# Sums of batches 5 and 6 ahead of the projection and scores of batch 7, and small steps moved to other engines

## The reference

```
xn  = layernorm(x)
qh, kh, vh = xn Wq^T, ctx Wk^T, ctx Wv^T
s   = causal(qh kh^T / 16);  p = softmax(s, axis=1)        # over the query axis
x1  = x + tanh(g_xattn) * (p vh)
xn2 = layernorm(x1)
xq  = clip(round(xn2 / sx)) ;  sx = sigmoid(clip_x) * max|xn2| / 127   # over all batches
h   = silu(xq Wg^T) * (xq Wu^T)      # weights quantised by row
out = x1 + tanh(g_ffn) * (quantised(h) Wd^T)
```

## Time and profile before

| | |
|---|---|
| median of the runs | 106.55 us |
| the profiled execution | 106.31 us |
| its span, first to last instruction | 104.5 us |
| TensorE clock granted | 1.00 throughout (the 2.4 GHz level) |
| PE busy | 96.9 us (93%) |
| DVE busy | 80.6 us (77%) |
| ACT busy | 66.1 us (63%) |
| POOL busy | 43.6 us (42%) |

### The profile page before, as it was taken

One profiled execution on the slowest core, in us unless ns is written; L12 is line 12 of the kernel. 1 busy time (PEld: TensorE's weight loads), 2 busy tenths in 40 slices (PEclk: granted clock), 3 DMA queues, 4 the chain that ended last, 5 costly groups with the idle time before them and its releaser, 6 DMA issues.

```text
span 104.5 us, 1739 instructions
## 1 busy us (share of the span) xinstructions
PE 96.9 (93%) x562; PEld 75.1 (72%) x564; DVE 80.6 (77%) x210; ACT 66.1 (63%) x125; POOL 43.6 (42%) x78
## 2 busy tenths in 40 slices
PE   7799999999999999999999987999999697899990
PEld 2268988988889898897878975444444386889970
DVE  0544296497998999597597979559999998879991
ACT  0421071657972755636738978789888989799800
POOL 6030335047083583508517594055696560350000
PEclk9999999999999999999999999999999999999999
DMA  2999999999354010010985500000000000005555
GB/s 51 333 371 336 376 422 419 419 407 401 138 6 44 0 45 9 23 34 0 150 154 116 110 0 0 0 6 3 0 0 0 0 0 0 0 6 192 209 201 201
DMA packets 11176, 13.54 MB, mean 130 GB/s; under 512 B 6432, under 2 KB 7712, under 8 KB 11168
## 3 DMA queue, kind: packets, MB, share of 16 engines
q1 hardware_dynamic: 10304, 12.39, 37.9%
q10 hardware_dynamic: 864, 1.05, 3.2%
HBM read 10.09 MB, written 2.10 MB: 117 GB/s over the span
## 4 chain that ended last, share of the span: by engine, by line
PE 47%; DVE 20%; DMA 16%; POOL 5%; issue 4%; ACT 3%; SPq 1%; DVEq 0%; POOLq 0%
PE ps L465 9%; DVE hmax L1100 9%; PE ps L686 9%; DMA spread<-rstd 8%; PE ps L503 5%; PE ps L485 5%; DMA r_wide<-spread 5%; DMA wk_sb<-in_wk 4%; DVE shared L1095 4%; PE ps L635 2%; POOL shared L436 2%; PE ps L523 2%; PE ps L540 2%; PE ps L691 2%; PE ps L516 2%
## 5 line engine op out<-in xcount | busy, mean ns | idle before, releaser
L635 PE MATMUL ps<-xq,wguT 128*128 128x512 bf16 x78 | 17.2, 379 | 0.7 <-DVE xq L1075 0.6
L436 POOL TENSOR_TENSOR shared<-up_sb,silu 128x1024 f32<-128x1024 f32 x5 | 11.8, 2366 | 9.5 <-ACT up_sb L830 9.5
L635 PEld LDWEIGHTS ps<-xq,wguT 128*128 128x128 bf16 x80 | 7.8, 98 | 9.8 <-issue 0.6
L465 PE MATMUL ps<-wvT,shared 128*128 128x256 f32 x56 | 13.3, 381 | 0.0
L485 PE MATMUL ps<-shared,a_sb 128*128 128x256 f32 x56 | 13.2, 379 | 0.0
L1100 DVE TENSOR_REDUCE hmax<-shared 128x1 f32<-128x2048 f32 (+1 forms) x6 | 12.7, 2109 | 0.6
L825 ACT ACTIVATE silu<-ps,gu_scale 128x1024 f32<-128x1024 f32 x10 | 11.2, 1115 | 2.1 <-PE ps L635 2.1
L503 PEld LDWEIGHTS ps<-uT,shared 128*128 128x128 f32 x64 | 10.7, 190 | 2.2 <-DVE uT L892 1.0
L503 PE MATMUL ps<-uT,shared 128*128 128x256 f32 (+1 forms) x64 | 12.0, 330 | 0.2 <-DVE uT L892 0.2
L465 PEld LDWEIGHTS ps<-wvT,shared 128*128 128x128 f32 x56 | 10.6, 190 | 1.8 <-DMA shared<-in_xc 0.4
L686 PE MATMUL ps<-hq,wdT 128*128 128x256 bf16 x80 | 10.6, 273 | 0.3 <-DVE hq L1135 0.3
(11 more groups left out here) (120 smaller groups left out, 188.4 us busy)
## 6 DMA issues: line engine op xcount, KB each, us to landing
shared<-in_xc SPq DMA_DIRECT2D x6, 512.0 KB, 10.8
out<-xn SPq DMA_DIRECT2D x7, 256.0 KB, 2.0
xs<-in_x SPq DMA_DIRECT2D x3, 512.0 KB, 8.4
shared<-in_wgu SPq DMA_DIRECT2D x3, 512.0 KB, 7.8
wd<-in_wd SPq DMA_DIRECT2D x1, 896.0 KB, 11.8
shared<-in_xc SPq DMA_DIRECT2D x3, 256.0 KB, 6.9
xs<-in_x ACTq DMA_DIRECT2D x2, 256.0 KB, 5.4
r_wide<-spread SPq DMA_DIRECT2D x4, 128.0 KB, 4.7
```

The source lines that it names most:

```text
L436: nc.gpsimd.tensor_tensor(hid[:, 2 * i + 1, :], up_sb[i % 2][:], silu1[i % 2][:], ALU.mult).then_inc(hid_done[1], 1)
L465: last = nc.tensor.matmul(values_bank(b, k), ctxT(b)[:, e, k * P:(k + 1) * P], weights[:, e, :], start=(e == 0), stop=(e == KT - 1))
L635: last = nc.tensor.matmul(bank(4 * half + 2 * g + c), wguT[:, i, g, k, :], xq[:, k, col:col + CH], start=(k == 0), stop=(k == KT - 1))
```

## The change

It has five parts, all in the handling of batches 5, 6 and 7.

1. TensorE: `attend` of 5 stands before the projection of 7, and `attend` of 6 before the scores of 7. Transposes of batch 0 stand between the identity products and the sum of 7.
2. VectorE: residual and statistics of 5 ahead of the scaled queries of 7, residual and statistics of 6 ahead of the row maximum of 7.
3. GpSimd forms `neg_dev` of batch 6 instead of ScalarE, and VectorE takes its largest value ahead of the statistics of 7, not behind them.
4. ScalarE makes the second half of the down weights' integers after the values of 6 and casts that half itself; GpSimd casts the first half alone.
5. SyncE issues the DRAM writes of batches 6 and 7 before the broadcast reads of both.

```diff
-            for b in range(WIDE_FROM, B):
+            def deviation_to_dram(b):
                 n = b - WIDE_FROM
                 sp.wait_ge(rstd1_done, b + 1)
-                sp.dma_start(spread[n], rstd1[:, b]).then_inc(spread_out, 16)
-                sp.wait_ge(spread_out, 16 * (n + 1))
+                sp.dma_start(spread[n], rstd1[:, b]).then_inc(spread_out[n], 16)
+
+            def deviation_to_all(b):
+                n = b - WIDE_FROM
+                sp.wait_ge(spread_out[n], 16)
...
+            for b in range(WIDE_FROM, LAST - 1):
+                deviation_to_dram(b)
+                deviation_to_all(b)
+            deviation_to_dram(LAST - 1)
+            deviation_to_dram(LAST)
+            deviation_to_all(LAST - 1)
+            deviation_to_all(LAST)
...
# GpSimd
-                    pool.wait_ge(wdint_done, KT)
-                    nc.gpsimd.tensor_copy(wd_q[:], wd_i16[:]).then_inc(wd_q_done, 1)
+                    pool.wait_ge(wdint_done, 1)
+                    nc.gpsimd.tensor_copy(wd_q[:, 0], wd_i16[:, 0]).then_inc(wd_q_done[0], 1)
...
+            pool.wait_ge(mv2_done, LAST)
+            for t in range(QT):
+                nc.gpsimd.tensor_scalar(neg_dev[:, t, :], xs[:, NT - 2 * QT + t, :], mv2[:, LAST - 1, t, 0:1], -1.0,
+                                        ALU.subtract, ALU.mult).then_inc(neg_dev6_done, 1)
...
# TensorE
             scores(LAST - 1)
+            attend(LAST - 2)
             project_queries(LAST)
-            attend(LAST - 2)
+            attend(LAST - 1)
             scores(LAST)
-            attend(LAST - 1)
             values_tile(LAST, 1).then_inc(v_done, 1)
...
+            transposes2(0)
             pe.wait_ge(exp_done, B)
...
-            for b in (0, 1, 2, 4, 5):
+            for b in (1, 2, 4, 5):
                 transposes2(b)
...
# ScalarE
-                if b == 5:
-                    quantise_down_weights(1)
             exponentials(LAST - 1)
             values_out(LAST - 1)
+            quantise_down_weights(1)
+            act.wait_ge(wdint_done, KT)
+            nc.scalar.copy(wd_q[:, 1], wd_i16[:, 1]).then_inc(wd_q_done[1], 1)
...
-            act.wait_ge(mv2_done, LAST)
-            for t in range(QT):
-                nc.scalar.activation(neg_dev[:, t, :], xs[:, NT - 2 * QT + t, :], ACT.Identity,
-                                     bias=mv2[:, LAST - 1, t, 0:1], scale=-1.0).then_inc(neg_dev_done, 1)
...
# VectorE
             row_max(LAST - 1)
             largest2(LAST - 3)
+            residual(LAST - 2)
+            invert_sum(LAST - 1)
+            stats2(LAST - 2)
             scale_queries_whole(LAST)
-            invert_sum(LAST - 1)
-            residual(LAST - 2)
-            stats2(LAST - 2)
             variance2(LAST - 2)
+            residual(LAST - 1)
+            stats2(LAST - 1)
             row_max(LAST)
+            variance2(LAST - 1)
...
-            residual(LAST - 1)
-            stats2(LAST - 1)
-            variance2(LAST - 1)
             largest2(LAST - 2)
...
+            dve.wait_ge(neg_dev6_done, QT)
+            largest_deviation(0, QT)
```

More of the change, by code:

```diff
@@ L225, in gated_block @@
         rbc_ready = sem("rbc_ready")
-        spread_out = sem("spread_out")
+        spread_out = [sem(f"spread_out{b}") for b in range(WIDE_FROM, B)]
         r_wide_here = [sem(f"r_wide_here{b}") for b in range(WIDE_FROM, B)]
@@ L258, in gated_block @@
         wdint_done = sem("wdint_done")
-        wd_q_done = sem("wd_q_done")
+        wd_q_done = [sem(f"wd_q_done{t}") for t in range(KT)]
+        neg_dev6_done = sem("neg_dev6_done")
         wguT_here = sem("wguT_here")
@@ L342, in _ @@
                                        wgu_q[:, s].rearrange("p n d -> p (n d)")).then_inc(wguT_here, 16)
-            sp.wait_ge(wd_q_done, 1)
             for t in range(KT):
+                sp.wait_ge(wd_q_done[t], 1)
                 sp.dma_start_transpose(wdT[:, :, t * P:(t + 1) * P], wd_q[:, t]).then_inc(wdT_here, 16)
@@ L418, in _ @@
                 pool.wait_ge(rstd2_done, b + 1)
-                pool.wait_ge(neg_dev_done, QT * (b - LAST + 2))
+                if b == LAST - 1:
+                    pool.wait_ge(neg_dev6_done, QT)
+                else:
+                    pool.wait_ge(neg_dev_done, QT)
                 for t in range(QT):
@@ L1037, in _, with largest_deviation @@
                 nc.vector.reciprocal(inv_sum[:, LAST, k:k + 1], row_sum[:, LAST, k:k + 1]).then_inc(inv_sum_done, 1)
-            residual(LAST - 1)
-            stats2(LAST - 1)
-            variance2(LAST - 1)
             largest2(LAST - 2)
+            def largest_deviation(n0, n1):
+                nc.vector.tensor_reduce(xmax[:, B - 2 + n0:B - 2 + n1], neg_dev[:, n0:n1, :], AX.X, ALU.max,
+                                        apply_absolute_value=True).then_inc(xmax_done, n1 - n0)
+            dve.wait_ge(neg_dev6_done, QT)
+            largest_deviation(0, QT)
             for t, bk in enumerate((RB, SC)):
@@ L1047, in _ @@
                 nc.vector.bn_aggr(mv2[:, LAST, t, :], bn2[:, LAST, t, :]).then_inc(mv2_done, 1)
[L1048 to L1051, removed]
+            for t in range(QT):
+                dve.wait_ge(neg_dev_done, t + 1)
+                largest_deviation(QT + t, QT + t + 1)
             dve.wait_ge(xmax_done, B - 2 + 2 * QT)
```

## The result

The changed kernel took 107.39 us (median of 8 runs, 106.73 to 108.01), the kernel before 106.38 us (8 runs). The ratio is 1.0095 with a 95% interval of 1.0073 to 1.0117: slower by 1.0 us. The forecast was 106.2 us, and the range ended at 107.1. The profiled execution's span is 105.4 us against 104.5.

What follows compares the result with a forecast made beforehand. TensorE was taken as last at the max product's barrier; closing its gap gains 0.49 at best, 0.33 with a 0.06 wait and 0.10 load. Taking 0.38 from 106.31 gives 105.93, plus 0.24 makes 106.2 us; range 105.6 to 107.1.

Steps and rivals of the forecast that it cites:

- the term for GpSimd's new pair: GpSimd's two instructions for the deviations of 6: 0.96 us together, 1.10 as upper bound, from 56.24 to 57.2 or 57.35.
- The cover: Time between the end of GpSimd's pair and VectorE's largest-value step of 6 at 57.49: 0.14 to 0.29 us.
- The slow-pair rival: GpSimd's pair at 0.82 us each, VectorE 0.39 late, gain 0.1, 106.45 us; chance 0.24 shared with another rival.
- the prediction's last 0.36 us: From GpSimd's inverse deviation of 7 ending at 60.37, over the final maximum (60.40 to 60.68), to TensorE's start at 60.73.
- the no-change side: Outcome that the kernel's time reads as the same, within about 0.5% (0.53 us); chance 0.55.
- the late broadcast: Rival: write of 7 and transposes slow the broadcast of 6 to 7.1 us, everything 1.1 later, 107.3 us; chance 0.12.
- The gain of 0.38: Whole kernel: forecast saving in us, taken between 0.49 at best and 0.33; chance of the forecast 0.54.
- TensorE was the last, by 0.14 us: Barrier before the max product at 61.21: VectorE's largest values were done at 61.07, GpSimd's inverse deviation at 60.46.
- TensorE's gap of 0.49 us: Around the scores of 7: they began 0.39 us late and exposed a weight load, 1.41 instead of 1.30; at most 0.49 gained.
- TensorE's stop before the sum of 7 and the exposed load: TensorE waiting for batch 7's first values tile, 57.15 against 57.14: a stop of some 0.06 us and 0.10 of load.
- Nothing is given back there: Behind the max product: first silu loses 0.1 of the gain, but the second waits for TensorE and times the rest.
- The thinnest cover: Values of 6 on ScalarE have their first tile at 52.30, the sum of 6 wants it at 52.37: 0.07 us.

Runs made afterwards that it cites:

- e0: Kernel before plus sixteen GpSimd instructions at the end of its stream, eight operation pairs each twice on 128x256 f32; 108.74 us in one run.
- e1: Changed kernel with GpSimd forming mean minus x as x times -1 plus the mean; 106.44 us, ratio to before 0.9971 to 1.0030.
- e9: e1 with the transposes of batch 0 back behind the sum of 7; 106.52 us, ratio to before 0.9995 to 1.0041.
- e7: Kernel before with the fifth part alone, both DRAM writes first; 106.35 us, ratio to before 0.9984 to 1.0020.
- e8: e1 with statistics of 6 split around the row maximum of 7 and transposes of batch 2 behind the max product; 106.37 us.
- e5: e1 with the DRAM writes and broadcasts of 6 and 7 in their old order; 106.37 us, ratio to before 0.9986 to 1.0029.

## Why the prediction was wrong

**The step that failed** is the term for GpSimd's new pair: "I take 0.96, the same form, with 1.10 as the upper bound". It measured 2.28. The form in the code was a subtract and a multiply; the rows that I took for "its neighbours" were add with multiply, and multiply with multiply. No row of the trace showed a subtract on GpSimd, so neither number was a bound. The operation was in the diff, and I matched the rows by size and number of columns alone. e0 and e1 settle it. The cover was 0.14 to 0.29 us; at 2.28 VectorE waited 1.05 us, and 0.86 of that reached the max product (13.99 against 13.13 in e1). The prediction's own sign of being wrong, a pair of over 0.6 us each, came true.

**The slow-pair rival named this mechanism** and underpriced it. At 0.82 us each it gave 106.45. The same working with 1.14 each puts VectorE 1.0 us late, its statistics of 7 at 60.34, and with GpSimd's 1.06 us and the prediction's last 0.36 us behind them the max product at 61.76: 0.55 us slower. Measured are 0.71 (13.99 against 13.28), and the time from GpSimd to VectorE, 0.14 and not 0.03 us, is most of the rest. I had filed the rival on the no-change side and left the slower side to the late broadcast. That one was wrong: scores of 6 start at 47.99, so the broadcast of 6 was in time with the write of 7 and the transposes beside it.

**The gain of 0.38 wasn't there either**, and e1, which has the pair at the time that I had worked out, shows it apart from the first error: 0.15 us at the max product, 0.06 at the second silu, nothing in the runs. Beside e0's lengths it is 0.04 and less than nothing, so no gain is shown. Three readings were wrong.
- Who was last at the barrier. The prediction read "TensorE was the last, by 0.14 us" from VectorE's end at 61.07 and the max product at 61.21. The 0.14 was no slack of VectorE's: it is the time from VectorE's end to TensorE's start. In every trace but e9's the max product starts 0.14 to 0.16 us after VectorE's last row, whatever TensorE had to do, and the kernel before is one of them:

```profile
60.99 0.08 DVE L1054 DVE_READ_ACCUMULATOR2_ANT col_max<- 128x1 f32 x1
```

  By e9's 0.45 us, which is the two warming products' four passes of 0.108, TensorE was ready at 60.67 + 0.45 = 61.12, 0.09 ahead of its start. So VectorE held the barrier in the kernel before already, and closing TensorE's gap of 0.49 us could gain only as much as VectorE gained with it. e7 (0.5 us less on TensorE, 0.10 gained), e8 (0.43 less, 0.01 gained) and e0 (the broadcast came sooner, scores of 7 0.22 us earlier, max product 0.11) agree.
- TensorE's stop before the sum of 7 and the exposed load are 0.22 us; I had 0.06 and 0.10 at most. I had ScalarE's signal reach TensorE in 0.05 us; in e1 the tile ends at 57.05 and the product starts at 57.19. The sum of 7 feeds VectorE's statistics, so this delay is on VectorE's path: counted from the scores of 6, they are done 0.22 us later than worked out.
- GpSimd's inverse deviation ends the wait of the final maximum, which starts 0.15 us after it ends, where I had 0.03. With the 0.22 us this makes 0.34 for the start of the final maximum (worked out 60.40, in e1 60.74 on the same count) and 0.33 for the max product (60.73, 61.06).

**The fifth part** was given the whole of the gap, 0.39 and 0.10 us. In the new orders it is worth nothing (e5), since there the broadcast has landed by 51.0 even in the old order (issued at 46.8, 4.2 us at most) and the projection of 7 ends at 52.4; alone on the kernel before no gain can be measured (e7).

**Behind the max product**: "Nothing is given back there" was wrong by 0.1 us. From the max product to the second silu it was 5.57 before and 5.66 in e1: ScalarE's last two conversions now wait 0.39 us for the last transposes and VectorE's last clip 0.30 us for them, and that clip is an input of the second half. The waits are in the trace; that they are the 0.1 us is argued.

**What was right**: the scaled queries of 7 end their wait on TensorE (52.68, worked out 52.62), the residual of 6 (53.96, 53.87), the row maximum of 7 (55.41, 55.35), the exponentials (55.86, 55.78), no cost of ScalarE's cast (0.94 us). The thinnest cover, 0.07 us ahead of the sum of 6, cost TensorE 0.04. Up to the one instruction whose duration came from the wrong row, VectorE's steps held within 0.1 us.

## What to carry to other kernels

When an operation moves to another engine, look for a row of that engine with that very operation; a row of the same shape with another operation is no bound, and where none exists the range must be wide and the wait for it must not stand at the head of a busy queue. When a gap on the busiest engine closes, ask what releases the next two engines once it is gone: here VectorE stopped waiting for the DMA and waited for TensorE's sum instead, 0.13 us earlier. And when two engines meet at a barrier, add the time of the signal before saying which was last: an end 0.14 us ahead of a start looked like slack and was the whole handover.

## What the hardware did that I had not expected

On GpSimd, one instruction on 128x256 f32 from memory to memory took 1.14 to 1.41 us with a subtract in either place of a two-operation instruction, and 0.40 to 0.76 us with multiply and add alone (e0; in the same place 1.14 in the changed kernel and 0.47 in e1). Mean minus x costs 2.4 times as much written as (x - mean) times -1 as it does written as x times -1 plus the mean. On VectorE the kernel before subtracts a column from a tile of the same size (L953) in 0.35 us. The Trainium skill (GPSIMD Engine Reference, section 4.1, Engine selection) calls one-input elementwise work on GpSimd roughly line-rate; beside VectorE's 0.35 us the trace agrees roughly for multiply and add (0.47), and not for subtract (1.14).
